# A residual of two adapted layers on Trainium2: adapter stack of 128 rows, first token sums and halves earlier, late adapter terms in other banks

## The chip, the cores and the metric

The kernel is written by hand, with a queue of instructions for each engine, and runs on one core of a Trainium2 chip. A core has TensorE (PE, with its weight loads shown as PEld), VectorE (DVE), ScalarE (ACT), GpSimd (POOL) and SyncE (SP), which here only issues DMAs. They meet at semaphores. The metric is the device time of one execution in microseconds (us), lower is better.

## The reference

Two layers, each added to its input. The first is a linear layer whose weight is quantised in groups of 128 against a codebook of 8 levels, with a low-rank term on both sides of the quantisation; the second is a gated MLP with an adapter chosen for each sequence.

```python
def layer0(x, weight, scale_log, codebook, lora_A, lora_B):       # weight 1024 x 1024, rank 64
    lora_delta = lora_B @ lora_A * (32.0 / 64.0)
    cb = codebook / clip(max(abs(codebook)), 1e-08)
    scale = exp(scale_log)
    normalized = (weight + lora_delta).reshape(O, I // 128, 128) / scale
    thresholds = (cb[:-1] + cb[1:]) * 0.5
    quantized = cb[searchsorted(thresholds, normalized, side='left')]
    w_eff = (quantized * scale).reshape(O, I) + lora_delta
    return x @ w_eff.T

def layer1(x, W_gate, W_up, W_down, A_*, B_*, lora_indices):      # H 1024, F 2752, rank 16, 16 adapters
    def lora_add(base, inp, A, B):
        Ab, Bb = A[0][lora_indices], B[0][lora_indices]           # one adapter for each of 8 sequences
        t = einsum('bri,bni->bnr', Ab, inp)
        return base + einsum('bor,bnr->bno', Bb, t) * 0.5
    gate = lora_add(x @ W_gate.T, x, A_gate, B_gate)
    up = lora_add(x @ W_up.T, x, A_up, B_up)
    act = silu(gate) * up
    return lora_add(act @ W_down.T, act, A_down, B_down)

x = x + layer0(x, ...)          # x is 8 x 256 x 1024, float32
x = x + layer1(x, ...)
```

## The kernel before

**The three stages.** Operands are split in two parts, high and low (names ending in h and l, as `xh`, `xl`), and each product is three matmuls: high by high, low by high, high by low. The token axis of 2048 is cut in NC = 4 pieces of 512, the feature axis of 1024 in KD = 8 tiles of 128. The first stage, up to about 239 us of the profiled span, quantises the eight row blocks of the first weight on VectorE (`quantise(o)`), transposes them on PE and makes 32 main products (`main(i)`, L1876), one for each block o and token piece c, in the order of the list ORDER. ScalarE copies each out of PSUM (`out_x1(i)`), and SyncE stores it to XR_d in DRAM (`store_x1(i)`). Product 26, for (7, 0), is LAST0, and 27, for (7, 1), is LAST1: their results go straight into the token tile `xr` too (L1095). The main products end at 239 us.

The second stage, 239 to 1190 us, makes gate and up by a scheme of seven products of half size in place of eight. A step u is one of them: mm = u // 7 counts the blocks of 128 output features (44 of them, gate and up in turn: m = mm % 2), p = u % 7 is the product. Each product is 12 matmuls of 512 columns (L1744). The scheme needs sums of token halves (`x_sum(n)`, L1323, four of them, from raw loads of XR_d into seven slots of `xr`) and sums of weight pieces (on GpSimd). `OUT` gives the PSUM bank of each product: bank1, bankA's second and first half, bank7, bank5, bankC's second and first half. `take(mm, p)` on VectorE reads them after products 2, 3, 4 and 6 of a block (L1269 to L1285), four reads in all, into `ev`. The stage runs twice, for tokens of halves h = 0 (u = 0 to 153) and h = 1 (u = 154 to 307). The third stage, 1190 us to the end, multiplies with W_down by the same scheme (L1967), reading its operands back from DRAM.

**The adapters.** The adapter projections of the tokens, `ts`, and the adapters' other factors, `bs`, are stacked in three groups of CR = 32 rows: one matmul with 96 rows adds the term to a product's bank (`lora`, L1760; 160 of them). In the first block pair of each half `ts` is not ready in time, as it comes from the first reads of PSUM themselves (`ts_mask`, L1341, L1348). There the terms are made later in banks of their own and added on VectorE (`late_lora`, L1768; `late_add`, L1355; 16 in all): before products 6, 7, 8, 9 and 13 to 16 of the half, in bank7, bank5 and the two halves of bankC. `td` (L1785) makes the down-projection's adapter term from `ah` and `al`, the high and low part of the activations, and `ad`.

**What sets the order.** Each engine's program is written out by hand. What stands behind a waiting instruction on an engine waits too; this holds for SyncE's and ScalarE's DMA issues. Between the first two stages the order matters most. BdT_d in DRAM holds an adapter matrix transposed in eight blocks; ScalarE copies a block from PSUM into the one buffer `bd_st` (`bd_copy(o)`, L1102) and may do so only when SyncE's store of the block before (`store_bd(o)`, L676) has landed. `load_raw` (L508) loads tokens from XR_d into slots of `xr`; `load_wn` and `load_wa` bring the rows of W_gate and W_up and their adapter rows; `w_tr(mm, n)` transposes them on VectorE, `hi(v)` and `lo(v)` split the weights of product v on ScalarE and VectorE (L951, L1245), `x_hi` and `x_lo` those of the tokens (L964, L1254), and `b_hi`, `b_lo` those of `bs`.

**The head.** `lb` holds a block of lora_B. SyncE loads lb(0) as its second load; PE transposes it (`lb_group(0)`, L1799), VectorE makes `lbT` of it and only then computes the thresholds from the codebook (from L1480). PE multiplies `la` by `lbT` (`lora_delta`, L1809), adds, transposes the quantised weights (`w_groups`, L1845) and the tokens (`nat_group`, L1828), and ScalarE and VectorE split both (`lxh`, `lxl`; `lwh`, `lwl`).

## Time and profile before

| | |
|---|---|
| Time, median of 3 runs | 1616.69 us (1616.1 to 1617.36) |
| The profiled execution's own time | 1616.32 us |
| Span of the profiled execution | 1614.7 us |
| PE busy | 1576.9 us, 98% of the span |
| DVE, ACT, POOL busy | 1275.1, 564.9 and 529.0 us |
| DMA | 257.13 MB, 159 GB/s in the mean |

The span goes from the first to the last instruction in the trace of one execution. All times within the profile are us from the span's start. The other times are of executions without a profile. Busy shares are means over three stages; what bounds a stage is read from the stage. A row of the page or the trace names the engine, the line in the kernel, the operation, the tile written, `<-`, and the tiles read. A wait in brackets is the engine's idle time just before the row, with what ended it.

### The profile page before, as it was taken

The page shows a single profiled execution, that of the slowest core. Times are in us where ns is not written, and L with a number is a line of the kernel's source. Part 1 is how long each engine was busy: PE and PEld are TensorE (multiplying, and loading weights), DVE is VectorE, ACT ScalarE, POOL GpSimd, SP SyncE. Part 2 cuts the span into 40 slices and gives each one's busy share as a digit, 9 for nine tenths or more (in the row PEclk, how much of TensorE's full clock was granted, in tenths as well). Part 3 has the DMA queues.
Part 4 walks back from the last instruction along what each step waited for, and adds up shares of the span by engine and source line. Part 5 has one row for each costly group of instructions (what it writes and reads, how often), then busy time and mean ns, then how long its engine had stood idle before and what let it go on. Part 6 is the DMA issues. An engine that isn't in the chain of part 4 may idle for free.

```text
span 1614.7 us, 21155 instructions
## 1 busy us (share of the span) xinstructions
PE 1576.9 (98%) x6968; PEld 1293.7 (80%) x6968; DVE 1275.1 (79%) x1674; ACT 564.9 (35%) x990; POOL 529.0 (33%) x399
## 2 busy tenths in 40 slices
PE   6999998999999999997999999999999999999999
PEld 4888886788888888876788888888888888888887
DVE  7998959988878988889887889989775576785443
ACT  6411134433333333354333333333343333233231
POOL 4410013455555555543444555555410000000000
PEclk9999999999999999999999999999999999999999
DMA  9552162565667777682446777776367777686563
GB/s 296 121 112 77 52 200 44 137 168 154 163 149 170 180 178 173 164 289 69 108 103 139 181 178 179 180 180 156 82 205 205 163 182 191 147 227 205 155 189 119
DMA packets 362444, 257.13 MB, mean 159 GB/s; under 512 B 219616, under 2 KB 283360, under 8 KB 362208
## 3 DMA queue, kind: packets, MB, share of 16 engines
q1 hardware_dynamic: 278784, 220.99, 52.2%
q10 hardware_dynamic: 81472, 28.99, 7.4%
q0 software_dynamic: 2080, 5.80, 1.7%
q8 instruction: 57, 0.93, 0.2%
q14 instruction: 51, 0.42, 0.1%
HBM read 165.74 MB, written 87.26 MB: 157 GB/s over the span
## 4 chain that ended last, share of the span: by engine, by line
PE 50%; DVE 1%; issue 0%; DVEq 0%
PE bank L1744 10%; PE bank L1967 9%; PE bankC L1967 6%; PE bankA L1744 6%; PE bankC L1744 6%; PE bankA L1967 6%; PE bankT L1967 3%; PE bankT L1785 1%; PE bankT L1786 1%; PE bankC L1760 1%; DVE ql L1417 0%; PE bank L1760 0%; PE bankA L1760 0%; DVE ev L1365 0%; DVE ll L1423 0%; DVE rl L1245 0%
## 5 line engine op out<-in xcount | busy, mean ns | idle before, releaser
L951 ACT CAST rh<-wt 128x512 fp32r<-128x512 f32 x308 | 190.7, 621 | 435.2 <-PE bankC L1760 127.7
L1245 DVE TENSOR_TENSOR rl<-wt,rh 128x512 fp32r<-128x512 f32 x308 | 274.0, 894 | 9.5 <-ACT rh L951 9.1
L1423 DVE TENSOR_TENSOR ll<-ll,lh 128x512 fp32r<-128x512 f32 (+1 forms) x154 | 107.8, 701 | 155.3 <-ACT lh L1060 155.0
L1744 PE MATMUL bank<-xh,rh 128*128 128x512 f32 x528 | 206.2, 391 | 1.1 <-issue 1.1
L1744 PE MATMUL bank<-xl,rh 128*128 128x512 f32 x528 | 205.8, 390 | 0.0
L1744 PE MATMUL bank<-xh,rl 128*128 128x512 f32 x528 | 205.7, 390 | 0.0
L1060 ACT CAST lh<-ll 128x512 fp32r<-128x512 f32 (+1 forms) x154 | 95.6, 621 | 268.6 <-DMA ll<-LT_d 263.5
L817 POOL TENSOR_TENSOR wt<-wt 128x512 f32<-128x512 f32 x44 | 60.1, 1365 | 321.6 <-DVE wt L1239 321.6
L1744 PE MATMUL bankC<-xh,rh 128*128 128x512 f32 x352 | 140.0, 398 | 3.1 <-DVE xl L1254 1.8
L1239 DVE STREAM_TRANSPOSE wt<-wn 128x512 f32<-128x512 f32 x176 | 124.1, 706 | 20.9 <-DMA wn<-Ag_d 9.0
L1744 PE MATMUL bankC<-xl,rh 128*128 128x512 f32 x352 | 139.5, 396 | 0.0
L1744 PE MATMUL bankC<-xh,rl 128*128 128x512 f32 x352 | 139.3, 396 | 0.0
L1744 PE MATMUL bankA<-xl,rh 128*128 128x512 f32 x352 | 137.0, 389 | 0.0
L1744 PE MATMUL bankA<-xh,rl 128*128 128x512 f32 x352 | 137.0, 389 | 0.0
L1744 PE MATMUL bankA<-xh,rh 128*128 128x512 f32 x352 | 137.0, 389 | 0.0
L1744 PEld LDWEIGHTS bank<-xh,rh 128*128 128x128 f32 x528 | 99.2, 188 | 23.1 <-issue 1.9
L1744 PEld LDWEIGHTS bank<-xl,rh 128*128 128x128 f32 x528 | 99.3, 188 | 21.2
L1744 PEld LDWEIGHTS bank<-xh,rl 128*128 128x128 f32 x528 | 99.1, 188 | 21.2
L830 POOL TENSOR_TENSOR wt<-wt 128x512 f32<-128x512 f32 x44 | 64.1, 1456 | 151.7 <-issue 91.2
L1269 DVE TENSOR_TENSOR ev<-bankA,tm 128x1024 f32<-128x1024 f32 x44 | 53.3, 1211 | 47.3 <-PE bankA L1760 45.7
L1967 PE MATMUL bank<-ql,lh 128*128 128x512 f32 (+1 forms) x231 | 90.0, 389 | 0.0
L1967 PE MATMUL bank<-qh,lh 128*128 128x512 f32 (+1 forms) x231 | 89.9, 389 | 0.0
(205 smaller groups left out, 3570.3 us busy)
## 6 DMA issues: line engine op xcount, KB each, us to landing
ll<-LT_d SPq DMA_DIRECT2D x148, 256.0 KB, 2.9
wn<-in_L_cond_W_gate_dram SPq DMA_DIRECT2D x80, 256.0 KB, 5.2
wn<-in_L_cond_W_up_dram SPq DMA_DIRECT2D x80, 256.0 KB, 5.1
RT_d<-dt SPq DMA_DIRECT2D x70, 256.0 KB, 3.2
ql<-RT_d SPq DMA_DIRECT2D x70, 256.0 KB, 3.8
LT_d<-ev ACTq DMA_DIRECT2D x60, 256.0 KB, 2.5
dn<-in_L_cond_W_down_dram SPq DMA_DIRECT2D x86, 128.0 KB, 3.8
LT_d<-s2a SPq DMA_DIRECT2D x40, 256.0 KB, 4.3
```

What stands on the lines that cost most here:

```text
L817: tt(wsrc(S1, rows), wsrc(L21, rows), wsrc(L22, rows), ALU.add).then_inc(s_sum, 1)
L830: tt(wsrc(L12, rows), wsrc(L12, rows), wsrc(S2, rows), ALU.subtract).then_inc(s_sum, 1)
L951: nc.scalar.copy(rh[:, v % RING, 0:KH * rows], wsrc(RSRC[p], rows)).then_inc(s_hi, 1)
L1060: nc.scalar.copy(lh[0:rows, n % NL, :], ll[0:rows, n % NL, :].bitcast(f32)).then_inc(s_lh, 1)
L1239: dv.transpose(wsrc(n, rows), src).then_inc(s_tr, 1)
L1245: dv.tensor_tensor(rl[:, v % RING, 0:KH * rows], wsrc(RSRC[p], rows), rh[:, v % RING, 0:KH * rows].bitcast(f32), ALU.subtract).then_inc(s_ ...
L1269: dv.tensor_tensor(e[:, 0:2, :], bankA[r, :, :], tm[r, None, :].to_broadcast([r.stop, 2, CH]), ALU.add).then_inc(s_ev, 1)
L1423: dv.tensor_tensor(ll[0:rows, n % NL, :], ll[0:rows, n % NL, :].bitcast(f32), lh[0:rows, n % NL, :].bitcast(f32), ALU.subtract).then_inc(s ...
L1744: last = te.matmul(OUT[p], a[:, u % RING, cols], b[:, OPND[p], k, :], start=k == 0 and n == 0, stop=k == KH - 1 and n == 2 and (p in (0, 1 ...
L1760: te.matmul(OUT[p][0:rows, :], bs[0:3 * CR, m, t, half * rows:(half + 1) * rows], ts[0:3 * CR, t, m, :], start=False, stop=True).then_inc( ...
L1785: te.matmul(bankT[:, :], lhs, ah[0:rows, :], start=begin, stop=False)
L1967: last = te.matmul(out_, a[0:rows, n % NL, tok], b[0:rows, k, :], start=(k == 0 and i == 0), stop=(k == NJ - 1 and i == 2))
```

## The change

It has five parts.

1. **Stack of 128 rows.** `lora` and `late_lora` multiply all 128 rows of `ts` and `bs`. Rows 96 to 127 are set to zero once, by GpSimd, at step u = 1; the first late term waits for it (semaphore s_z).
2. **Head.** lb(0) is loaded on ScalarE's queue, ahead of all else on it, instead of SyncE's. VectorE computes the thresholds before it makes lbT. PE does `w_groups(0)` before `lora_delta(1)`, and VectorE splits the first block's weights at the beginning of the next `quantise` instead of after its scaling.
3. **Seam between stage one and two.** The numbering of the token sums changes so that the first sum needs LAST0 alone, not LAST1. SyncE issues three raw loads before the store of BdT block 6. ScalarE asks for the first adapter rows earlier, and splits products 3 and 4 earlier; VectorE likewise, ahead of the first token sum, and transposes two weight pieces of block 1 before the token splits.
4. **Late terms.** They come before products 8, 9, 11, 12 and 14 to 17 of the half, the first four in bankC and bankA. The first activations' silu is at product (1, 6) instead of (1, 4), and copies, splits and `td` of the first block pair come one product later.
5. **Stage three** keeps its operands in one pair of tiles, `oph` and `opl`, with tables L_AT and R_AT for the places; what is read and multiplied stays.

The core of the diff:

```diff
+        LATE_BANK = ((bankC[0:FH, 1, :], bankC[0:FH, 0, :], bankA[0:FH, 1, :], bankA[0:FH, 0, :]),
+                     (bank7[0:FH, :], bank5[0:FH, :], bankC[0:FH, 1, :], bankC[0:FH, 0, :]))
+        LATE_AT = {8: (0, 0), 9: (0, 1), 11: (0, 2), 12: (0, 3), 14: (1, 0), 15: (1, 1), 16: (1, 2), 17: (1, 3)}
...
-        XORD = R11, T2, R21, T3, T1, T4, R22 = range(7)
+        XORD = R11, T2, R21, T3, T1, T4, R22 = (0, 4, 2, 3, 1, 5, 6)
@@ SyncE @@
-                load_lb(0)
...
-                store_bd(KD - 2)
-                stored(sp, TURN[KD - 2, 1] + 1)
+                stored(sp, KH * NC)
                 load_raw(0, 0, KH, 0, s_x[0])
                 load_raw(1, 0, KH, 3, s_x[3])
+                stored(sp, TURN[KD - 2, 0] + 1)
+                load_raw(0, KH, KD - 1, 2, s_x[2])
+                store_bd(KD - 2)
                 store_x1(LAST1)
+                stored(sp, TURN[KD - 2, 1] + 1)
                 load_raw(1, KH, KD - 1, 6, s_x[6])
-                load_raw(0, KH, KD - 1, 2, s_x[2])
+                load_wn(1)
                 store_bd(KD - 1)
                 store_x1(TURN[KD - 2, 2])
-                load_wn(1)
@@ GpSimd @@
+                    if u == 1:
+                        stored(gp, NORD)
+                        gp.wait_ge(s_bdst, 16 * KD)
+                        gp.wait_ge(s_sum, 4)
+                        gp.memset(ts[3 * CR:P, :, :, :].bitcast(f32), 0.0).then_inc(s_z, 1)
+                        gp.wait_ge(s_z, 2)
+                        gp.memset(bs[3 * CR:P, :, :, :].bitcast(f32), 0.0).then_inc(s_z, 1)
@@ ScalarE @@
+                for i in range(NI):
+                    act.dma_start(lb[i * Q:(i + 1) * Q, :, :],
+                                  lora_B[i * DI:i * DI + Q, None, :].to_broadcast([Q, 2, RL])).then_inc(s_lb0, 16)
...
                                 w_hi(o)
+                                if o == KD - 1:
+                                    load_wa(0)
...
                 bd_copy(KD - 2)
-                load_wa(0)
                 hi(0)
                 out_x1(LAST0)
                 hi(1)
                 out_x1(LAST1)
+                x_hi(0, 0)
                 bd_copy(KD - 1)
                 b_hi(0)
                 hi(2)
+                hi(3)
+                hi(4)
                 load_wa(1)
                 out_x1(TURN[KD - 2, 2])
-                x_hi(0, 0)
-                hi(3)
@@ VectorE @@
-                        dve.wait_ge(s_main, LAST1 + 1)
+                        dve.wait_ge(s_main, LAST0 + 1)
...
                 lo(2)
+                lo(3)
+                lo(4)
                 x_sum(0)
                 x_lo(0, 0)
                 for n in range(1, 4):
                     x_sum(n)
+                w_tr(1, 0)
+                w_tr(1, 1)
@@ PE @@
-                te.matmul(OUT[p][0:rows, :], bs[0:3 * CR, m, t, half * rows:(half + 1) * rows], ts[0:3 * CR, t, m, :],
+                te.matmul(OUT[p][0:rows, :], bs[:, m, t, half * rows:(half + 1) * rows], ts[:, t, m, :],
...
+                    if h == 0 and m == 0:
+                        pe.wait_ge(s_z, 3)
-                    pe.wait_ge(s_ev, 4 * 2 * NJ * h + 4 * m + (2, 3, 4, 4)[i])
+                    pe.wait_ge(s_ev, 4 * 2 * NJ * h + ((4, 4, 5, 5), (6, 7, 8, 8))[m][i])
...
-                lora_delta(1)
                 w_groups(0)
+                lora_delta(1)
...
-                    if first(it) and 7 * m + p in (6, 7, 8, 9, 13):
-                        late_lora(h, (7 * m + p - 6) // 7, (7 * m + p - 6) % 7)
-                    if it % NJ == 1 and m == 0 and p < 3:
-                        late_lora(h, 1, p + 1)
+                    if u % (14 * NJ) in LATE_AT:
+                        late_lora(h, *LATE_AT[u % (14 * NJ)])
```

**SyncE's DMA issues at the first seam.** XR_d<-x1t_st stores a main product, BdT_d<-bd_st a block of BdT, and xr<-XR_d is a raw load. Before:

```order
L681 DMA XR_d<-x1t_st 128x512 [waits s_x1t]
L676 DMA BdT_d<-bd_st 128x128 [waits s_bd]
L508 DMA xr_93<-XR_d 128x4x512 [waits s_x1tst1,s_x1tst0]
L508 DMA xr_93<-XR_d 128x4x512
L681 DMA XR_d<-x1t_st 128x512 [waits s_x1t]
L508 DMA xr_93<-XR_d 128x3x512 x2
L676 DMA BdT_d<-bd_st 128x128 [waits s_bd]
L681 DMA XR_d<-x1t_st 128x512 [waits s_x1t]
```

Now:

```order
L683 DMA XR_d<-x1t_st 128x512 [waits s_x1t]
L511 DMA xr_93<-XR_d 128x4x512 [waits s_x1tst1,s_x1tst0]
L511 DMA xr_93<-XR_d 128x4x512
L511 DMA xr_93<-XR_d 128x3x512 [waits s_x1tst1,s_x1tst0]
L678 DMA BdT_d<-bd_st 128x128 [waits s_bd]
L683 DMA XR_d<-x1t_st 128x512 [waits s_x1t]
L511 DMA xr_93<-XR_d 128x3x512 [waits s_x1tst1,s_x1tst0]
L468 DMA wn_97<-in_L_cond_W_up_dram 32x3x256 [waits p1_tr]
```

The store of BdT block 6 has moved from before the first raw load to behind the third, and the four loads now stand in the order of slots 0, 3, 2, 6.

**ScalarE at the same seam.** bd_st<-bankC is the copy of a block of BdT, rh<-wt a weight split, x1t_st<-bank the copy of a main product, xh<-xr a token split, wn<-Au_d the request for adapter rows. Before, from the copy of product (7, 1) on:

```order
L1095 COPY xr_93<-bankT 128x512 [waits s_x1tst1,s_main]
L1096 COPY x1t_st<-bankT 128x512
L1102 ACTIVATE bd_st<-bankC 128x128 [waits s_bdst,s_trM]
L983 ACTIVATE bh<-bt 128x192 [waits p1_bt]
L951 CAST rh<-wt 128x512 [waits p1_tr]
L974 DMA wn_97<-Au_d 32x2x256 [waits p1_tr]
L974 DMA wn_97<-Au_d 32x2x256 x3
L1096 COPY x1t_st<-bank 128x512 [waits s_x1tst0,s_main]
```

Now:

```order
L1110 COPY xr_93<-bankT 128x512 [waits s_x1tst1,s_main]
L1111 COPY x1t_st<-bankT 128x512
L976 CAST xh_91<-xr_93 128x1024 [waits p1_x0]
L976 CAST xh_91<-xr_93 128x1024
L1117 ACTIVATE bd_st<-bankC 128x128 [waits s_bdst,s_trM]
L995 ACTIVATE bh<-bt 128x192 [waits p1_bt]
L963 CAST rh<-wt 128x512 [waits p1_tr]
L963 CAST rh<-wt 128x512 [waits p1_sum] x2
L986 DMA wn_97<-Au_d 32x2x256 [waits p1_tr]
L986 DMA wn_97<-Au_d 32x2x256 x3
L1111 COPY x1t_st<-bank 128x512 [waits s_x1tst0,s_main]
```

The first token split stands ahead of the last copy into bd_st, and two more weight splits (x2) ahead of the adapter rows and the main product's copy.

**PE around the first late term**, from the last three matmuls of product 5 of the half. Before:

```order
L1744 MATMUL bankC<-xh_91,rh 128x512
L1744 MATMUL bankC<-xl_92,rh 128x512
L1744 MATMUL bankC<-xh_91,rl 128x512
L1768 MATMUL bank<-ts,bs 96x512 [waits p1_bs0,p1_ev,p1_tlo,p1_ts]
L1744 MATMUL bankC<-xh_91,rh 128x512 [waits p1_xlo,p1_lo]
L1744 MATMUL bankC<-xl_92,rh 128x512
L1744 MATMUL bankC<-xh_91,rl 128x512
```

Now, that place and the first late term, which comes behind product 7 (bank<-xh,rh and so on):

```order
L1764 MATMUL bankC<-xh_91,rh 128x512
L1764 MATMUL bankC<-xl_92,rh 128x512
L1764 MATMUL bankC<-xh_91,rl 128x512
L1764 MATMUL bankC<-xh_91,rh 128x512 [waits p1_xlo,p1_lo]
L1764 MATMUL bankC<-xl_92,rh 128x512
L1764 MATMUL bankC<-xh_91,rl 128x512
L1764 MATMUL bankC<-xh_91,rh 128x512
```

```order
L1764 MATMUL bank<-xh_91,rh 128x512
L1764 MATMUL bank<-xl_92,rh 128x512
L1764 MATMUL bank<-xh_91,rl 128x512
L1790 MATMUL bankC<-ts,bs 96x512 [waits p1_bs0,p1_tlo,p1_ev,p1_ts,p1_z]
L1764 MATMUL bankA<-xh_91,rh 128x512 [waits p1_ev,p1_lo]
L1764 MATMUL bankA<-xl_92,rh 128x512
L1764 MATMUL bankA<-xh_91,rl 128x512
```

The matmul of ts and bs has gone from before product 6 to before product 8, writes bankC instead of bank (bank7), and has one wait more (p1_z).

## Rows read from the trace of the kernel before

**Rows 1.** The page, part 1: busy us of each engine, share of the span, instructions.

```profile
PE 1576.9 (98%) x6968; PEld 1293.7 (80%) x6968; DVE 1275.1 (79%) x1674; ACT 564.9 (35%) x990; POOL 529.0 (33%) x399
```

**Rows 2.** Waits, whole span: engine, line, waited for: us, times, longest us.

```profile
ACT bd_st L1102 <- DMA BdT_d<-bd_st: 9.4, 2, 7.5
...
PE bank L1768 <- DVE ts L1348: 9.2, 2, 5.9
...
PE bankC L1799 <- DMA lb<-in_L_cond_lora_B_dram: 9.1, 1, 9.1
...
PE bankT L1785 <- DVE al L1329: 3.8, 4, 1.6
...
PE bank L1768 <- ACT ts L1000: 0.6, 1, 0.6
```

**Rows 3.** Windows: length, busy us (instructions) of five engines, granted clock, DMA share, GB/s.

```profile
34.00:36.00 2.00, 1.41 (x3) 1.16 (x4) 0.50 (x2) 0.00 (x0) 0.00 (x0) 0.54 1.05 379
262.90:266.20 3.30, 3.29 (x8) 2.62 (x9) 3.24 (x5) 1.35 (x3) 0.00 (x0) 0.50 0.26 43
```

**Rows 4.** Windows, two stretches of steady matmuls, same columns.

```profile
820.00:1020.00 200.00, 200.00 (x879) 165.01 (x878) 170.46 (x223) 70.43 (x125) 101.41 (x70) 1.00 0.69 157
1300.00:1500.00 200.00, 200.00 (x882) 165.41 (x882) 139.88 (x223) 66.99 (x115) 0.00 (x0) 1.00 0.70 188
```

**Rows 5.** Timeline of PE around a 96-row matmul: start us, us.

```profile
848.23 0.40 PE L1760 MATMUL bank<-ts,bs 96*128 96x512 f32 x1
...
849.16 0.39 PE L1744 MATMUL bankC<-xh,rh 128*128 128x512 f32 x1
```

**Rows 6.** Timeline of the head, ScalarE and PE: waits stand in brackets.

```profile
33.27 0.59 ACT L1081 CAST lxl<-bankC 128x512 fp32r<-128x512 f32 x1
...
34.59 2.08 PE L1809 MATMUL bank<-la,lbT 128*128 128x512 f32 x4 [1.36 <-DVE lbT L1457]
...
40.07 0.47 PE L1876 MATMUL bank<-lxh,lwh 128*128 128x512 f32 x1 [1.15 <-DVE lwl L1575]
```

**Rows 7.** Timeline of SyncE's queue, its DMA issues at the seam.

```profile
216.74 0.97 SPq L508 DMA_DIRECT2D xr<-XR_d  x2
...
220.45 0.99 SPq L508 DMA_DIRECT2D xr<-XR_d  x2
...
221.49 0.51 SPq L676 DMA_DIRECT2D BdT_d<-bd_st  x1
```

**Rows 8.** Tile BdT_d, 190 to 240 us: time from issue to landing.

```profile
DMA to landing us min/median/max: 2.1/2.1/10.7
```

**Rows 9.** Tile xr, 210 to 240 us: time from issue to landing.

```profile
DMA to landing us min/median/max: 5.9/9.6/11.1
```

**Rows 10.** Timeline of the first seam, by time, several engines.

```profile
211.66 0.39 PE L1876 MATMUL bankT<-lxh,lwh 128*128 128x512 f32 x1
...
214.71 0.58 ACT L1095 COPY xr<-bank 128x512 f32<-128x512 f32 x1
...
219.60 0.53 POOL L912 MEMSET ad<- 128x512 f32 x1
...
219.93 0.29 ACT L1102 ACTIVATE bd_st<-bankC 128x128 f32<-128x128 f32 x1
...
227.11 2.29 DVE L1323 TENSOR_TENSOR xr<-xr 128x2048 f32<-128x2048 f32 x1 [5.40 <-DMA xr<-XR_d]
...
268.51 1.23 DVE L1285 TENSOR_TENSOR ev<-bankC,ev 128x1024 f32<-128x1024 f32 x1
...
270.75 0.40 PE L1744 MATMUL bankA<-xh,rh 128*128 128x512 f32 x1
```

**Rows 11.** Timeline of the second half's seam, VectorE and PE.

```profile
734.88 3.67 DVE L1254 TENSOR_TENSOR xl<-xr,xh 128x1024 fp32r<-128x1024 f32 x2
...
748.43 1.23 DVE L1285 TENSOR_TENSOR ev<-bankC,ev 128x1024 f32<-128x1024 f32 x1
...
750.99 0.40 PE L1744 MATMUL bankA<-xh,rh 128*128 128x512 f32 x1
```

More of the change, by code:

```diff
@@ L735, in _ @@
                     late_b = it % NJ in (0, 1)
-                    if m == 0 and 0 < it < NIT and p == (3 if it % NJ == 1 else 0):
+                    if m == 0 and 0 < it < NIT and p == (4 if it % NJ == 1 else 0):
                         store_bs(it, 1)
@@ L1167, in _ @@
                         a_hi(4 * it)
-                    if 0 <= it - 1 < NIT and first(it - 1) and (m, p) == (0, 1):
+                    if 0 <= it - 1 < NIT and first(it - 1) and (m, p) == (0, 2):
                         a_hi(4 * (it - 1))
@@ L1965, in _ @@
                         out_ = BANK2[r % 2][t]
-                        for i, (a, b) in enumerate(((lh, qh), (lh, ql), (ll, qh))):
-                            last = te.matmul(out_, a[0:rows, n % NL, tok], b[0:rows, k, :],
+                        for i, (a, b) in enumerate(((oph, oph), (oph, opl), (opl, oph))):
+                            last = te.matmul(out_, a[0:rows, L_AT[n % NL], tok], b[0:rows, R_AT[k], :],
                                              start=(k == 0 and i == 0), stop=(k == NJ - 1 and i == 2))
```

107 lines of the change are left out of this document (55 added, 52 removed).

## The prediction

> **What bounds the kernel now.** I read the page's busy shares first: TensorE (PE) is busy for 98% of the span [rows 1], so a gain is a gap of PE closed, a clock kept up, or a cheaper matmul. The list of waits says where PE stands still: 9.1 us until lora_B lands at the start, and 9.2 us in two pieces (the longer 5.9) for the small adapter operand ts at the first late term of each half; further down 3.8 us for al; and ScalarE waits 9.4 us in two pieces for a store of BdT [rows 2]. The windows show that gaps of PE cost twice: after them the granted clock was 0.54 of full in 34 to 36 us and 0.50 for 3.3 us from 262.9, the lower level, 1.2 instead of 2.4 GHz [rows 3]. Last I compared PE's rate in two stretches without a wait: 882 matmuls in 200 us of the last matrix product, 879 in 200 us of the first, where the adapter products are [rows 4].
>
> **Change 1: the adapter product on 128 rows instead of 96.** After the 96-row matmul at 848.23 four starts take 0.93 us, to 849.16 [rows 5]; at the plain rate of 200/882 = 0.2268 us they would take 0.907: 0.023 us lost. The two rates agree with that: 3 matmuls x 0.2268 = 0.68 us in 200 us, over some 38 adapter products, is 0.018 each, and the last product has 96-row steps of its own that lose some as well; I take 0.025. There are 160 regular and 16 late adapter products: 176 x 0.025 = 4.4 us (bounds 0, if the loss hangs on something else in these matmuls, and 5). The Trainium skill ("TensorE: Matmul & The Clock Gate", LDWEIGHTS) says that a 32x128 weight load takes as long as a 128x128 one, only columns count. By that rule this part is worth nothing; the trace doesn't decide on the load, but shows starts that slip behind the matmul.
>
> **Change 2: the head.** lora_B now leads ScalarE's queue, and VectorE makes its constants while it travels, instead of after it. Four issues fewer stand ahead of the codebook on SyncE, and the first quantisation should end some 2.5 us earlier. But PE's next work also needs ScalarE's splits of the tokens, which end at 33.27 + 0.59 = 33.86 [rows 6]: these, not VectorE, will be last. The tokens come four issues (some 0.5 us each, as on SyncE [rows 7]) later on ScalarE's queue, and today PE waits for them a little; so 33.86 slips by up to 1 us. Today four delta matmuls and 16 transposes run from 34.59 to about 39, at half clock, and the first main matmul comes at 40.07, after a wait of 1.15 for VectorE's last split of the weights [rows 6]. With the quantised weights there earlier, their transposes and that split go ahead of the delta. I take 40.07 - 1.15 for the wait that goes, less 0.7 of today's 1.36 ahead of 34.59: 38.2, a gain of 1.8 us (bounds -0.5, the tokens' delay, and 2.9, both waits and 0.4). PE is busy without a gap worth naming from there to 239 us, so the shift is kept.
>
> **Change 3: the seam between the two layers (200 to 313 us).** Here VectorE decides. The first token sum starts at 227.11, when its two loads land, and VectorE is never idle from there to the end of the fourth PSUM read at 268.51 + 1.23 = 269.74: 42.6 us [rows 10]. The change takes two weight splits out of this stretch (1.2 us), leaving 41.4, and starts the loads when main product (7,0) is done, at 211.66 [rows 10]. Today ScalarE copies it at 214.71, behind a cast that waits for weight transposes, and these for the adapter rows, whose request now goes out earlier. From that copy to the load's issue at 216.74 [rows 7] are 2.03 us, 0.5 of it the BdT store between: 211.7 + 0.3 + 1.5 gives 213.6, 3.1 us earlier.
> What SyncE's order shows speaks against the gain: the store of BdT (o = 6), which stood ahead of the loads, now stands behind three of them. A BdT store with little ahead landed in 2.1 us, the one issued at 221.49 behind the loads in 10.7 [rows 7, 8]. ScalarE's next copy into bd_st waits for that store, and ScalarE works in order. The last load, issued at about 220.97, took 11.1 [rows 7, 9], so 3.5 MB went from 216.74 to about 232.1, 4.4 us per MB; the three ahead of the store are 2.75 MB: 213.6 + 12.1 = 225.7, the store at 226.3. Today that copy ran at 219.93 [rows 10]. Queued behind it on ScalarE are b_hi(0), hi(2), hi(3), hi(4), the next adapter rows and out_x1. Who waits: VectorE's b_lo(0), lo(2), lo(3), lo(4), all ahead of the first sum, and through out_x1(28) PE's main product 30. After the copy (0.3) come a cast of 0.4 and three of 0.5, and one split (0.7): the first sum starts at 229.0, 1.9 us later than today. If ScalarE weren't held it would start with its loads at 213.6 + (227.11 - 216.74) = 224.0.
> From 229.0, 41.4 us of VectorE's work: 270.4. The new zeroing of ts and bs on GpSimd (512 elements took 0.53 us [rows 10]; 3072 make some 3.2) runs beside it and may slow VectorE by 0 to 1.6; I take 0.5: 270.9. PE now needs exactly this read before the late term ahead of product 8, so that product starts at 271.2 where today it is 270.75 [rows 10]: 0.45 lost. The wait ahead of product 6 is gone, but PE stands about as long ahead of 8, and the half clock then falls on work that nothing hides: a spell of 3.3 us [rows 3] loses up to half its length, I take 1.2 us. Behind product 8 there are gains: the silu no longer stands ahead of the adapter copies on ScalarE (0.6, the third wait for ts [rows 2]), and the down-projection terms come one product later, which covers 1.6 of the 3.8 us for al [rows 2]. Sum: -0.45 - 1.2 + 0.6 + 1.6 = 0.6 gained (bounds -3 and 6.5).
>
> **Change 4: the same seam in the second half (712 to 790 us).** No load moves. Today PE waits 5.9 us for ts [rows 2]; now product 6 starts when its token split ends, 734.88 + 3.67 = 738.6 [rows 11]. But VectorE's chain to the read at 748.43 + 1.23 = 749.66 stays, and the late term now waits for it: product 8 starts at 749.9 instead of 750.99 [rows 11], 1.1 gained. The gap of 5.9 becomes one of 3.5 and one near 5, after which I expect the half clock once where nothing hides it (1.4, a little more, the gap being longer). Behind it one wait for al of the four (0.9) and some slack at the late terms (0.4): 1.1 + 1.3 - 1.4 = 1.0 us (bounds -1.5 and 3).
> The tiles of the last product only change places; nothing of their order moves: 0.
>
> **Sum**, against the profiled execution's own 1616.32 us (span 1614.7 and 1.6 around it): -4.4 - 1.8 - 0.6 - 1.0 = -7.8, so 1608.5. It lies 0.4 under the median of the timed runs (1616.69), so **1608.9**.
>
> **Rivals.**
> - A, the forecast: ScalarE is held by the BdT store. For it: 10.7 against 2.1 us [rows 8]. Chance 0.45.
> - B: the store lands in time, or little waits for it. The first sum starts at 224.0, 5.0 us earlier: 1603.9. Against it: the two landings. Chance 0.25.
> - C: the 96 rows are not what makes the starts slip; the 4.4 are missing: 1613.3. Against it: the slip sits right behind the 96-row matmul [rows 5]. This is also what the skill's rule, quoted above, would give. Chance 0.13.
> - D: the head gives nothing or loses 0.5, since the tokens land late behind lora_B, with the hold of A: 1610.7 to 1611.2. Chance 0.12.
> - E, slower: the hold of ScalarE grows. Place: the copy of BdT (o = 7) into bd_st. Price: one us of the whole for each us of landing past 226, for main product 30, all sums and the splits stand behind it. To eat 7.8 and 3.2 more the store must land after 237, which 2.75 MB do only at half of today's rate: 1620. Chance 0.05.
>
> The range 1602.5 to 1613.5 leaves out E, half of C and the best of B. This kernel's measurement tells about 0.2% (3.2 us) from no change, so faster means under 1613.5. A (0.44 of 0.45), B (0.25), half of C (0.06) and most of D (0.10) are faster: 0.85; the rest of C and D and an edge of A 0.10; slower 0.05.
>
> **What would show it.** In the profile after: starts behind adapter matmuls at 0.227 us, and as many matmuls per 200 us as in the last product (else C). First main matmul at 37.5 to 39, no wait of 9 us. ScalarE's copy into bd_st waiting for a BdT store until about 224.5, the first sum near 227 (B: near 222), both 1.8 under the clock of before by the head, then a wait of PE for the PSUM read ahead of the first late term. In the second half a wait of PE that ends near 749.9 less the total shift. I would be wrong if main matmuls wait earlier than 200 us, or if the waits for al and ad grow.

## The result, and the profile after

The changed kernel takes 1629.98 us (median of 4 runs, 1629.51 to 1631.03); the kernel before, run beside it, 1617.03. The ratio is 1.0081 (95% interval 1.0066 to 1.0096): 13 us slower, where I had forecast 8 us faster. In the profiled executions it is 1630.23 against 1616.32 us, 13.9 more, and their spans differ by as much:

```profile
span 1628.6 us, 21162 instructions
...
PE 1577.9 (97%) x6968; PEld 1295.6 (80%) x6968; DVE 1273.3 (78%) x1674; ACT 565.1 (35%) x990; POOL 526.8 (32%) x401
```

PE is busy 1.0 us more than before [rows 1] and stands still 12.9 us more; stretches at half clock count as busy. The starts of the products of stage two, read from PE's timelines, say where (a stretch ends with the start of the product named last, the rest with the span):

| stretch, by products u of stage two | its end before, us | its end after, us | lost (+) or gained (-) |
|---|---|---|---|
| to product 0: head and main products | 239.02 | 243.43 | +4.4 |
| 0 to 8 | 270.75 | 274.77 | -0.4 |
| 8 to 21 | 312.66 | 321.68 | +5.0 |
| 21 to 154, no seam | 714.40 | 721.67 | -1.7 |
| 154 to 162, start of the second half | 750.99 | 757.57 | -0.7 |
| 162 to 182 | 812.95 | 828.62 | +9.1 |
| 182 to 307, no seam | 1186.80 | 1200.62 | -1.9 |
| rest, stage three | 1614.7 | 1628.6 | +0.1 |

So there are three losses: one in the head, and one behind product 8 of either half. In the two stretches without a seam the change gains. PE's waits in the profile after name the same places (us in total, times, longest; "issue" is a wait for nothing that the profile shows):

```profile
PE bankT L1807 <- DVE al L1346: 9.9, 6, 3.4
...
PE bankA L1853 <- DMA nat<-in_x_dram: 6.8, 2, 5.5
...
PE bankC L1824 <- DMA lb<-in_L_cond_lora_B_dram: 6.5, 1, 6.5
...
PE bankC L1790 <- DVE ev L1302: 6.4, 2, 3.9
...
PE bankC L1764 <- issue: 4.5, 2, 3.2
```

The wait for lora_B fell from 9.1 [rows 2] to 6.5, but 6.8 us for `nat`, the tokens, are new. The waits for ts are gone and 6.4 us for `ev`, the read of PSUM, stand in their place. Those for `al` grew from 3.8 [rows 2] to 9.9.

**The head.** The queues of ScalarE and SyncE, and PE's first token transposes (start, duration, and in brackets the idle time and what ended it):

```profile
0.94 1.81 ACTq L1075 DMA_DIRECT2D lb<-in_L_cond_lora_B_dram  x4
...
4.68 1.01 ACTq L1080 DMA_DIRECT2D nat<-in_x_dram  x2
...
4.06 0.98 SPq L649 DMA_DIRECT2D nat<-in_x_dram  x2
...
16.48 1.08 PE L1853 MATMUL bankA<-ident,nat 128*128 128x128 f32 x4 [5.52 <-DMA nat<-in_x_dram]
...
40.03 1.88 PE L1870 MATMUL bankA<-ident,eff 128*128 128x128 f32 x8 [0.77 <-ACT lxl L1096]
...
44.26 0.47 PE L1901 MATMUL bank<-lxh,lwh 128*128 128x512 f32 x1
```

ScalarE's two loads of the first token piece went out at 4.68, behind eight other issues (2.77 in the kernel before), and SyncE's loads of the second piece already at 4.06 (6.00 before). These are the times from issue to landing of ScalarE's two loads after:

```profile
DMA to landing us min/median/max: 11.7/14.1/16.5
```

The first of them took 7.9 us before; it landed at 10.7 then and lands at 16.4 now, and PE stood 5.5 us for it. SyncE's first load landed at about 13.8, ahead of it. ScalarE's splits end at 39.9 instead of 33.9 us, and the first main product starts at 44.26 instead of 40.07 [rows 6].

**Behind product 8.** SyncE's queue, VectorE and PE in the first half:

```profile
262.19 1.80 SPq L472 DMA_DIRECT2D wn<-in_L_cond_W_gate_dram  x4
...
291.01 1.15 SPq L507 DMA_DIRECT2D bs<-bh  x2
...
294.73 2.07 SPq L472 DMA_DIRECT2D wn<-in_L_cond_W_up_dram  x4
...
295.71 0.68 DVE L1365 TENSOR_TENSOR ts<-tx,ts 32x512 fp32r<-32x512 f32 x1 [3.35 <-ACT ts L1011]
...
302.33 0.71 DVE L1256 STREAM_TRANSPOSE wt<-wn 128x512 f32<-128x512 f32 x1 [3.82 <-DMA wn<-in_L_cond_W_up_dram]
...
313.00 0.61 PE L1807 MATMUL bankT<-ah,ad 96*128 96x512 f32 x1 [3.36 <-DVE al L1346]
```

The stores into bs (L507, six DMAs that refill bs) wait for the late terms' additions of the first block, as those terms still read bs. It is by far SyncE's longest wait from 262 to 303 us (the kernel before has two there, the longer of 19.1 us):

```profile
SPq L502 <- DVE ev L1372: 26.9, 1, 26.9
```

The last of these additions now comes with product 12 instead of 9, and the stores go out at 291.01 where they went at 278.57 before. Behind them on SyncE stands the load of the next block of W_up: 294.73 where it was 282.29. VectorE's transposes wait 3.8 us for it, until 302.33, and all that VectorE has behind them is late: PE then waits 3.4 us for `al`. In the second half it is the same, and more: VectorE waits 5.9 us.

```profile
DVE wt L1256 <- DMA wn<-in_L_cond_W_up_dram: 9.7, 2, 5.9
...
DVE ts L1365 <- ACT ts L1011: 4.1, 2, 3.3
```

The same list of the kernel before has no wait for W_up. Its queue of SyncE at this place:

```profile
278.57 1.15 SPq L504 DMA_DIRECT2D bs<-bh  x2
...
282.29 2.06 SPq L469 DMA_DIRECT2D wn<-in_L_cond_W_up_dram  x4
```

**What came as forecast.** ScalarE's copy into bd_st waited for the store of BdT, which took 9.5 us from its issue at 219.38 to its landing, and the first token sum came behind it:

```profile
228.93 0.28 ACT L1117 ACTIVATE bd_st<-bankC 128x128 f32<-128x128 f32 x1 [3.65 <-DMA BdT_d<-bd_st]
...
233.06 2.28 DVE L1340 TENSOR_TENSOR xr<-xr 128x2048 f32<-128x2048 f32 x1
```

The starts behind an adapter matmul do not slip any more, and both stretches without waits now hold 883 matmuls in 200 us, where they held 879 and 882 [rows 4]:

```profile
820.00:1020.00 200.00, 200.00 (x883) 165.29 (x882) 169.30 (x223) 70.64 (x127) 100.75 (x70) 1.00 0.69 160
...
1300.00:1500.00 200.00, 200.00 (x883) 165.45 (x882) 142.25 (x228) 66.31 (x113) 0.00 (x0) 1.00 0.71 190
```

And PE's timeline around one of them, four starts in 0.91 us where it was 0.93 [rows 5]:

```profile
849.29 0.39 PE L1780 MATMUL bankC<-ts,bs 128*128 128x512 f32 x1
...
850.20 0.39 PE L1764 MATMUL bank<-xh,rh 128*128 128x512 f32 x1
```

The weight load of these matmuls (PEld; busy us, then mean ns of one) takes the same time with 96 rows, in the kernel before, as with 128 rows now:

```profile
L1760 PEld LDWEIGHTS bankC<-ts,bs 96*128 96x128 f32 x80 | 15.0, 188 | 3.1
...
L1780 PEld LDWEIGHTS bankC<-ts,bs 128*128 128x128 f32 x80 | 15.0, 188 | 3.1
```

### The profile page after: what moved, and what is told of

It reads as the page before. It is cut to its first block, busy times and chain, and to the rows that moved or that the text cites. A ratio compares the mean times of both kernels' runs of the same rounds, so it can differ in the third digit from the quotient of the medians.

```text
span 1628.6 us, 21162 instructions
## 1 busy us (share of the span) xinstructions
PE 1577.9 (97%) x6968; PEld 1295.6 (80%) x6968; DVE 1273.3 (78%) x1674; ACT 565.1 (35%) x990; POOL 526.8 (32%) x401
## 4 chain that ended last, share of the span: by engine, by line
PE 49%; DVE 1%; SPq 0%; DMA 0%; issue 0%; DVEq 0%
PE bank L1991 9%; PE bank L1764 9%; PE bankC L1991 6%; PE bankA L1991 6%; PE bankA L1764 6%; PE bankC L1764 6%; PE bankT L1991 3%; PE bankT L1807 1%; PE bankT L1808 1%; PE bankC L1780 1%; DVE opl L1433 0%; DMA bs<-bt 0%; PE bank L1780 0%; PE bankA L1780 0%; DVE opl L1439 0%; DVE ev L1381 0%
## 5 line engine op out<-in xcount | busy, mean ns | idle before, releaser
L1439 DVE TENSOR_TENSOR opl<-opl,oph 128x512 fp32r<-128x512 f32 (+1 forms) x154 | 107.4, 698 | 155.5 <-ACT oph L1072 155.2
L1072 ACT CAST oph<-opl 128x512 fp32r<-128x512 f32 (+1 forms) x154 | 95.5, 621 | 268.5 <-DMA opl<-LT_d 263.5
L1991 PE MATMUL bank<-opl,oph 128*128 128x512 f32 (+1 forms) x231 | 90.0, 390 | 0.0
L1991 PE MATMUL bank<-oph 128*128 128x512 f32 (+1 forms) x231 | 89.9, 389 | 0.0
```

The lines of the kernel that those rows point to most:

```text
L1072: nc.scalar.copy(oph[0:rows, L_AT[n % NL], :], opl[0:rows, L_AT[n % NL], :].bitcast(f32)).then_inc(s_lh, 1)
L1439: dv.tensor_tensor(opl[0:rows, L_AT[n % NL], :], opl[0:rows, L_AT[n % NL], :].bitcast(f32), oph[0:rows, L_AT[n % NL], :].bitcast(f32), ALU ...
L1991: last = te.matmul(out_, a[0:rows, L_AT[n % NL], tok], b[0:rows, R_AT[k], :], start=(k == 0 and i == 0), stop=(k == NJ - 1 and i == 2))
```

## The experiments

All ratios are against runs of the kernel before on the same chip, with 95% intervals. The kernel before took 1616.1 us in the median beside experiments 1 to 4, 1616.8 beside 5 to 8 and 1616.0 beside 9 to 11, so across these groups the ratios compare better than the times.

| | time, us | ratio |
|---|---|---|
| changed kernel | 1629.98 | 1.0081 (1.0066 to 1.0096) |
| 1, weight load ahead of the stores of bs | 1620.94 | 1.0024 (1.0015 to 1.0033) |
| 2, lora_B on SyncE | 1625.52 | 1.0056 (1.0042 to 1.0070) |
| 3, late terms at their old places | 1617.47 | 1.0008 (0.9999 to 1.0017) |
| 4, kernel before with 128 rows alone | 1613.27 | 0.9981 (0.9972 to 0.9990) |
| 5, 2 and 3 together | 1614.64 | 0.9987 (0.9978 to 0.9996) |
| 6, 5 and the store of BdT ahead | 1609.30 | 0.9958 (0.9945 to 0.9972) |
| 7, 1 and the silu behind ts | 1618.72 | 1.0010 (1.0001 to 1.0019) |
| 8, four mends, late terms at new places | 1611.50 | 0.9964 (0.9950 to 0.9978) |
| 9, 6 with the old order in the head | 1610.06 | 0.9959 (0.9945 to 0.9972) |
| 10, 6 with lora_B on ScalarE, tokens in order | 1608.48 | 0.9953 (0.9939 to 0.9966) |
| 11, kernel before with the zeroing alone | 1616.91 | 1.0005 (0.9996 to 1.0014) |

**1. The weight load ahead of the stores of bs**, on SyncE alone:

```diff
-                    if m == 1 and it + 1 < NIT and p == (3 if late_b else 0):
-                        store_bs(it + 1, 0)
                     if p == 3 and 0 <= mm + 2 < NM:
                         load_wn(mm + 2)
+                    if m == 1 and it + 1 < NIT and p == (3 if late_b else 0):
+                        store_bs(it + 1, 0)
```

> The changed kernel, with one swap on SyncE: where both fall at the same step, the load of the block after next of W_gate or W_up is issued before the six stores of the adapter operand bs, not behind them. Theory (the stores wait for late terms that now come up to three products later, and the weight load behind them comes 12 us late, so VectorE stands 3.8 and 5.9 us for it): both of these waits go, the products behind number 8 of each half come 4 to 5 us and 7 to 8 us earlier, and the time falls by 9 to 12 us, from 1630 to 1618 to 1621. Rival 1 (the silu and the down-projection's operands, one to two products later in the order, are what is late): the waits of VectorE for weights go, but PE's waits for al stay at about 3 us each, and the time falls by less than 3 us. Rival 2 (the new banks of the late terms, reads of PSUM in the way): no change.

9.0 us came back by one swap of two steps. The load of W_up goes out at 284.64 and VectorE does not wait for it any more; PE waits for `al` 6.4 us in eight pieces:

```profile
284.64 2.01 SPq L472 DMA_DIRECT2D wn<-in_L_cond_W_up_dram  x4
...
290.67 1.15 SPq L507 DMA_DIRECT2D bs<-bh  x2
```

```profile
PE bankT L1807 <- DVE al L1346: 6.4, 8, 1.8
```

The wait in the queue is the cause of the greater part. In the profile 3.8 us come back from product 8 to 21 and 4.4 from 162 to 182, where I expected 4 to 5 and 7 to 8: the second half is still 4.7 us behind the kernel before in that stretch. So Rival 1 has a share; the 3.8 us for `al` of the kernel before are not reached either.

**2. lora_B back on SyncE**, first in its queue behind lora_A:

```diff
-                for i in range(NI):
-                    act.dma_start(lb[i * Q:(i + 1) * Q, :, :],
-                                  lora_B[i * DI:i * DI + Q, None, :].to_broadcast([Q, 2, RL])).then_inc(s_lb0, 16)
...
                 sp.dma_start(qsum[0:RL, :], lora_A).then_inc(s_la, 16)
+                for i in range(NI):
+                    sp.dma_start(lb[i * Q:(i + 1) * Q, :, :],
+                                 lora_B[i * DI:i * DI + Q, None, :].to_broadcast([Q, 2, RL])).then_inc(s_lb0, 16)
```

> The changed kernel, with the first block of lora_B loaded as second load on SyncE's queue again, as in the kernel before; the order on VectorE and PE stays the changed one. Theory (the four issues ahead of ScalarE's tokens and the earlier token loads of SyncE's queue hand the DMA engines to the wrong tokens first, so the first ones land at 16.3 instead of 10.7 us): the first tokens land at 10.5 to 12 us, the first main product starts at 39 to 40.5 instead of 44.3 us, and the time falls by 4 to 5.5 us, to 1624.5 to 1626. Rival (PE's and VectorE's new order in the head costs it: transposes of weights ahead of the low-rank product): the first main product stays later than 43 us and the time within 1.5 us of 1630.

1625.5, the theory's time, in the median of six executions. One of them, which is the profiled one, took 4094 us; without it the median is 1624.9. Its profile, with 0.83 us for a matmul throughout, is not used, and the head is read from experiments 5, 6 and 10. They show that this edit does more than its theory says: it also puts lora_B ahead of the codebook again (experiment 5).

**3. Late terms at their old places**: part 4 of the change undone, its core being

```diff
-        LATE_AT = {8: (0, 0), 9: (0, 1), 11: (0, 2), 12: (0, 3), 14: (1, 0), 15: (1, 1), 16: (1, 2), 17: (1, 3)}
+        LATE_AT = {6: (0, 0), 7: (0, 1), 8: (0, 2), 9: (0, 3), 13: (1, 0), 14: (1, 1), 15: (1, 2), 16: (1, 3)}
```

> The changed kernel with part 4 undone in full: late terms before products 6, 7, 8, 9, 13 to 16 in bank7, bank5 and bankC, the silu at (1, 4), everything of the first block pair at its old place; stack of 128 rows, head and seam stay. Theory: product 8 of the first half a little later (the wait ahead of product 6 returns), but no wait of VectorE for weights at 298 and 780 us, and the whole at 1616 to 1619 (1630 less 4.6 and 8.5 us, less the gain of 128 rows that was counted in them, plus nothing). Rival (the swap alone gives it all back and the late terms' new places are worth something for themselves): this run is 1 to 3 us slower than the one with the swap.

12.5 us came back, 3.5 more than by the swap: beside the queue, something else in part 4 costs. Experiment 7 finds 2.2 of it in the silu. And with the wait ahead of product 6 back, the first half shows no gain of the seam's new order against the kernel before: product 0 starts 4.4 us later than there, product 8 4.5 and product 21 4.4. (Experiment 4, which has 128 rows and the old seam, needs 1.1 us more from product 0 to 21 than this one, but that loss is not explained, so it shows no gain either.) PE's gap ahead of product 6 is 5.0 us:

```profile
267.46 0.71 PE L1791 MATMUL bank<-ts,bs 128*96 128x512 f32 x1 [4.96 <-ACT ts L1012]
```

**4. 128 rows alone** in the kernel before: the matmuls of `lora` and `late_lora` on 128 rows, the zeroing and the wait for it.

```diff
-                    te.matmul(OUT[p][0:rows, :], bs[0:3 * CR, m, t, half * rows:(half + 1) * rows], ts[0:3 * CR, t, m, :],
+                    te.matmul(OUT[p][0:rows, :], bs[:, m, t, half * rows:(half + 1) * rows], ts[:, t, m, :],
```

> The kernel before, with the stack of 128 rows alone (rows 96 to 127 zeroed on GpSimd at step 1, the first late term waits for it). Theory (each 96-row matmul makes the starts behind it slip by 0.025 us, 176 of them): 1617.0 - 4.4 = 1612.6. Rival (in the head and at the seams VectorE sets the pace and takes part of it back, or GpSimd's zeroing slows VectorE at the seam): 1613.5 to 1615.

Faster by 2.9 us; the time lies between the theory's 1612.6 and the rival's 1613.5, and the interval (1.6 to 4.5 us) holds both. The gain per matmul is as forecast: from product 28 to 150 the kernel makes up 1.85 us against the one before, over 70 adapter matmuls, 0.026 each. But over the first seam (products 5 to 21) it loses 1.1 us again, 0.7 of it from product 6 to 7, and over the second (158 to 182) 0.5. In experiment 11, with the zeroing alone, the profile does not show this loss.

**5. Experiments 2 and 3 together.**

> The changed kernel with part 4 (late terms) undone in full and the first block of lora_B back on SyncE's queue: what stays of the change is the stack of 128 rows, the new order of PE and VectorE in the head, and the seam between the first two stages. Theory (parts add up): 1617.5 - 4.5 = 1613.0, the first product of stage two at 238.7 to 239.5 us, and PE's gap ahead of product 6 as with part 4 undone alone, near 5 us: the seam's new order gives nothing, as ScalarE is held by the store of BdT. Rival (the head's new order gives 1 us or more once the tokens land as early as before): first product of stage two before 238 us, 1612 or less.

1614.6, between theory and kernel before. Product 0 starts at 240.7; in experiment 6, the same in the head, at 239.0; the kernel before had 239.0 too. So the head's new order of VectorE and PE shows no gain at product 0 in either. The tokens are not the reason: ScalarE's first load landed at 11.4 us (10.4 in experiment 6, 10.7 in the kernel before), and PE does not wait for it. The new order computes the constants from the codebook ahead of lbT, and with lora_B back on SyncE the codebook stands behind it in the queue. VectorE waits for the codebook, and PE for lbT (in the kernel before, 0.7 us, and the token transposes at 12.17):

```profile
10.58 0.17 DVE L1491 SCALAR_TENSOR_TENSOR cbt<-cb 128x8 f32<-128x8 f32 x1 [3.90 <-DMA cb<-in_condB_codebook_dram]
...
12.91 2.07 PE L1835 MATMUL bank<-la,lbT 128*128 128x512 f32 x4 [3.19 <-DVE lbT L1473]
...
14.78 1.05 PE L1854 MATMUL bankA<-ident,nat 128*128 128x128 f32 x4
```

Experiment 6 has the same two waits, 2.6 and 3.8 us. Its head is without the stretch at half clock that this one has: here the granted clock was 0.50 from 38.1 to 41.4 us, there 1.00 from 30 to 48. Behind the head, ScalarE is held as forecast, and the first sum late:

```profile
226.06 0.28 ACT L1117 ACTIVATE bd_st<-bankC 128x128 f32<-128x128 f32 x1 [3.63 <-DMA BdT_d<-bd_st]
...
230.05 2.28 DVE L1340 TENSOR_TENSOR xr<-xr 128x2048 f32<-128x2048 f32 x1
```

**6. The store of BdT ahead of the raw loads**, and the first token split behind the weight splits:

```diff
                 store_x1(LAST0)
+                store_bd(KD - 2)
                 stored(sp, KH * NC)
...
                 load_raw(0, KH, KD - 1, 2, s_x[2])
-                store_bd(KD - 2)
...
-                x_hi(0, 0)
                 bd_copy(KD - 1)
                 b_hi(0)
                 hi(2)
                 hi(3)
                 hi(4)
+                x_hi(0, 0)
```

> As the run with part 4 undone and lora_B on SyncE, with the store of BdT block 6 issued ahead of the three raw token loads instead of behind them, and on ScalarE the first token split behind the weight splits 2, 3 and 4 instead of ahead of the copy into bd_st. Theory (ScalarE's wait for that store holds the weight splits and so the first token sum): the copy into bd_st doesn't wait, the first sum starts at 223.5 to 225 instead of about 228.6 us, PE's gap ahead of product 6 shrinks from 5 to under 1.5 us, and the time is 1608 to 1610.5. Rival 1 (the token loads, not the hold, set the first sum): the sum starts no earlier than 227 us, 1612 to 1613.5. Rival 2 (the sum starts earlier, but the chain to ts and the reads of PSUM is paced by PE's products): the gap shrinks by less than half, 1611 to 1612.

1609.3: 5.3 us less, by the two edits together; what each gives is not separated. The copy into bd_st waits no more and stands at 218.26, the first sum starts at 222.48, 7.6 us earlier than in experiment 5 (1.7 of it the head), and product 8 at 267.36 instead of 273.46:

```profile
218.26 0.30 ACT L1117 ACTIVATE bd_st<-bankC 128x128 f32<-128x128 f32 x1
...
222.48 2.29 DVE L1340 TENSOR_TENSOR xr<-xr 128x2048 f32<-128x2048 f32 x1
...
229.55 2.29 DVE L1340 TENSOR_TENSOR xr<-xr 128x2048 f32<-128x2048 f32 x1 [2.39 <-DMA xr<-XR_d]
...
259.58 0.71 PE L1791 MATMUL bank<-ts,bs 128*96 128x512 f32 x1 [4.08 <-ACT ts L1015]
```

The gap ahead of product 6 is still 4.1 us, not under 1.5 as the theory had it (rival 2 had that right, though not the time): product 5 ends earlier too, as its waits for token splits (1.6 and 0.4 us in experiment 5) are gone. The second sum now waits 2.4 us for its load.

**7. The silu behind the casts of ts**, added to experiment 1:

```diff
-                        if (m, p) == (1, 6):
-                            for n in range(3):
-                                silu(it, n)
                         if p in (4, 6):
                             ts_hi(it // NJ, m, p // 6)
+                        if (m, p) == (1, 6):
+                            for n in range(3):
+                                silu(it, n)
```

> The changed kernel with the weight load ahead of the stores of bs on SyncE, as in the first experiment (1620.9), and on ScalarE the three silu of the first block pair behind the two casts of ts at the same step, not ahead of them. Theory (the table load and three silu hold the cast that VectorE waits 3.3 us for, and that delay comes out at PE's waits for al): VectorE's wait for ts of 3.3 us at 292 to 296 goes, PE's waits for al shrink from 6.4 us in sum to under 4, time 1618 to 1619.5. Rival (the waits for al come from the order, gating and split one product later on a VectorE that is full): no change, 1620 to 1621.5.

1618.7, 2.2 less than experiment 1, with a wide scatter (1614.8 to 1620.0, and 1618.1 to 1623.5 there) and ratios whose intervals just overlap. The profiles agree on the direction: 1.6 us less from product 8 to 21 and 2.9 less from 162 to 182. VectorE's wait of 3.3 us for ts is gone and PE's waits for `al` are 3.9 us, as the theory had it. So the silu did hold the casts of ts at its new place. With the swap and this the ratio is 1.0010, where experiment 3, with the late terms at their old places, has 1.0008: a cost of the new places beyond the queue and the silu is not shown in these two.

**8. All mends, late terms at their new places**: experiments 7, 2, and the edit of 6.

> The changed kernel with its late terms at their new places and four mends: weight load ahead of the stores of bs, silu behind the casts of ts, lora_B on SyncE, store of BdT block 6 ahead of the raw loads. Theory (the late terms' new places cost by themselves, because PE's wait ahead of product 6 is split in two, ahead of 6 and of 8, and the half clock after the second falls on products that nothing hides): 2 to 4 us slower than the run with the same mends and the late terms at their old places, 1611 to 1614. Rival (with the weights in time and ts early, two products more of slack for ts are a gain): as fast as that run or faster, under 1609.

1611.5, 2.2 slower than experiment 6 in the medians, though the intervals of the ratios overlap; in the profiles 3.4, of which 1.6 are the head. At product 160 it is ahead of experiment 6 by 2.0 us, at 162 behind by 0.9, at 182 by 3.5:

```profile
734.24 0.47 PE L1764 MATMUL bankC<-xh,rh 128*128 128x512 f32 x1 [3.18 <-issue]
...
739.49 0.67 PE L1807 MATMUL bankT<-ah,ad 128*128 128x512 f32 x1 [2.26 <-DVE al L1346]
...
745.39 0.44 PE L1790 MATMUL bankC<-ts,bs 128*96 128x512 f32 x1 [0.87 <-DVE ev L1302]
...
793.32 0.47 PE L1807 MATMUL bankT<-ah,ad 96*128 96x512 f32 x1 [1.95 <-DVE al L1346]
```

The windows behind the second and the last of them, where the granted clock (third number from the end) is half:

```profile
739.60:743.00 3.40, 3.40 (x9) 2.66 (x10) 3.27 (x5) 1.67 (x3) 2.00 (x2) 0.50 0.21 80
...
794.30:797.60 3.30, 3.30 (x9) 2.53 (x9) 3.17 (x6) 0.43 (x1) 1.49 (x2) 0.50 0.20 60
```

The one wait of 5.9 us is now 3.2, 2.3 and 0.9, and at 791 there is another of 1.9 for `al`; after two of them the clock falls to half for 3.4 us. The time is the theory's, but its reason, the wait split ahead of 6 and 8, is not borne out: from product 158 to 162, over the three pieces, this version takes 21.8 us (two late matmuls come behind them now), where experiment 6 with its one wait and 6.8 us at half clock takes 22.2. It loses 2.6 us behind that, from product 162 to 182, where the wait of 1.9 us and the second window at half clock stand; experiment 6 has waits of 0.4 and 0.9 us there and its clock is full. In the first half, from product 0 to 154, this version is 0.3 us faster.

**9. The old order in the head**, added to experiment 6 (constants behind lbT, `lora_delta(1)` ahead of `w_groups(0)`, the weight split behind the scaling).

> The best run so far (128 rows, late terms at their old places, lora_B on SyncE, store of BdT ahead of the raw loads: 1609.3) with the head of the kernel before in full: constants of VectorE behind lbT, low-rank product of block 1 ahead of the transposes of block 0's quantised weights, weight split behind the scaling. Theory (the first main products hang on the tokens' landing and ScalarE's splits, and the new order adds nothing, or loses up to 1.5 us because the low-rank product that the second quantisation needs comes later): 1608 to 1609.5. Rival (the new order gives what I forecast once the tokens are early, 1 to 2 us): this run is slower, 1610.3 to 1611.3.

1610.1 against 1609.3: no difference that can be told. The time lies between the theory's range (to 1609.5) and the rival's (from 1610.3), and the ratios are 0.9959 and 0.9958. In the profile product 0 starts 0.7 us later than in experiment 6. Both have lora_B on SyncE, where the new order waits for the codebook; with lora_B on ScalarE the old order was not tried.

**10. lora_B on ScalarE as in the change, the second token piece behind the scales**, on the base of experiment 6:

```diff
-                load_nat(2)
-                load_nat(3)
                 for i in range(NI):
                     sp.dma_start(scale[i * Q:(i + 1) * Q, 1:KD, :],
                                  scale_log[i * DI + Q:(i + 1) * DI].rearrange("(o r) g u -> r o (g u)", r=Q)).then_inc(s_scr, 16)
+                load_nat(2)
+                load_nat(3)
```

> The best run so far, but with lora_B on ScalarE's queue ahead of everything, as the change has it, and on SyncE's queue the loads of the second token piece behind the four loads of the remaining scales instead of ahead of them. Theory (the first tokens landed late because SyncE's token loads, issued at 4.06 instead of 6.0 us, got ahead of ScalarE's, issued at 4.68 instead of 2.77; with those out of the way only the 1.9 us of the four issues stay): the first tokens land at 11.5 to 13.5 us instead of 16.3, stage two starts at 238.5 to 241, time 1609 to 1611.5. Rival (the four issues ahead of ScalarE's tokens cost it all): first tokens at 15.5 us or later, stage two at 243 us, 1613 to 1614.5.

1608.5, and the profiled execution 1606.6. ScalarE's token loads still go out at 4.68, behind eight issues; with SyncE's at 6.00 instead of 4.06, the first of them lands at 10.9 instead of 16.4 us, and PE starts on it without a wait at 10.97 instead of 16.48. The rival had 15.5 or later. ScalarE's two loads took, and around them stood:

```profile
DMA to landing us min/median/max: 6.2/7.8/9.5
...
4.68 1.02 ACTq L1080 DMA_DIRECT2D nat<-in_x_dram  x2
...
4.06 1.89 SPq L654 DMA_DIRECT2D scale<-in_L_cond_scale_log_dram  x4
...
6.00 1.32 SPq L649 DMA_DIRECT2D nat<-in_x_dram  x2
...
10.97 1.08 PE L1854 MATMUL bankA<-ident,nat 128*128 128x128 f32 x4
```

Product 0 starts at 235.75, 3.3 us earlier than in the kernel before and in experiment 6, and earlier than the theory's 238.5 to 241. Here the codebook is there before lora_B, and VectorE waits for neither. In the medians only 0.8 us of that show, with overlapping intervals: that this head is no worse than the old one is shown, that it is better rests on one profiled execution.

**11. The zeroing alone**, with 96 rows.

> The kernel before with 96 rows, and only GpSimd's zeroing of rows 96 to 127 of ts and bs at step 1 and the wait of the first late term for it. Theory (the zeroing runs beside VectorE and ScalarE at the seam and costs there what the stack of 128 rows alone missed, 1.0 of 4.4 us): PE's gap ahead of product 6 near 5 instead of 3.2 us, product 21 at 313.5 instead of 312.7, time 0.8 to 1.5 us above the kernel before. Rival (the loss comes from the 128 rows or from scatter): no difference, within 0.4 us.

The times cannot tell: the median is 0.9 us above the kernel before's, within the theory's range, but the interval reaches from 0.6 us faster to 2.3 slower. The profile speaks for the rival: the shift of 0.3 to 0.5 us is there from product 0 on and does not grow at the seam, and PE's gap ahead of product 6 is 3.3 us, not near 5. What experiment 4 loses at the seams is not settled; its wait ahead of product 6 is 4.9 instead of 3.2 us, and the half clock lasts 6.8 us in one piece that begins within this wait, instead of twice 3.4, one of them ahead of the wait.

## Why the prediction was wrong

- **Change 1, 4.4 us: right in mechanism.** -1.7 and -1.9 in the two stretches without a seam, at 0.026 a matmul (I took 0.025). Alone it measured 2.9, as 1.1 and 0.5 us are lost at the seams. The Trainium skill ("TensorE: Matmul & The Clock Gate", LDWEIGHTS) says that a weight load's time goes by its columns, not by its rows. The traces agree: 188 ns with 96 and with 128 rows. I wrote that the trace does not decide on the load; it did. And I was wrong that by this rule the part is worth nothing: the time is lost in the starts behind the matmul, not in the load, and there 883 matmuls fit in 200 us instead of 879. Why the starts slip stays open.
- **Change 2, -1.8 us: wrong, +4.4.** The step that failed is "33.86 slips by up to 1 us": it slipped by 6.0, to 39.9. I counted the issues on ScalarE's queue and took the landing to move with them. But I had noted myself that SyncE's queue gets shorter, and used it only for the codebook: its token loads, two of 1 MB (512 x 512 float32) that PE needs later, went ahead of ScalarE's by the same 1.9 us. The first tokens landed 5.7 us later. Rival D had the mechanism's place and a size of 0.5. Experiment 2 takes the loss away by putting lora_B back (4.5 to 5.1 us), experiment 10 by putting the other tokens back instead; in its profile the head then gains 3.3 us, more than the 1.8 that I forecast.
- **Change 3 up to product 8, 0.45 lost: right in mechanism.** The hold of ScalarE by the store of BdT was there (copy at 228.9 less 4.4 of the head is 224.5, where I had 226.3), the first sum at 233.06 less 4.4 is 228.7 (229.0 forecast, though the terms behind 226.3 add up to 229.2), product 8 at 270.4 (271.2 forecast, so 0.4 gained instead). Experiment 6 takes the hold away and gains 5.3 us, near the 5.0 of rival B, but its second edit has a share that is not known. The zeroing, for which I took 0.5 us, shows no cost at this seam in experiment 11's profile.
- **Change 3 behind product 8, 2.2 us gained: wrong, 5.0 lost. Change 4, 1.0 gained: wrong, 8.4 lost.** The step that failed is "Behind product 8 there are gains". I never followed the late terms to SyncE's queue, where `store_bs` waits for their additions, and the load of the weights stands behind it. SyncE's order has these stores and their wait for the additions at almost the same place as before; a wait whose row stays in place still gets longer when what it waits for moves. Experiment 1 shows 9.0 us for it. The silu was the smaller miss: that it "no longer stands ahead" was true of the first casts of ts alone (experiment 7, 2.2). The waits for `al` were to shrink by 1.6 and 0.9 us; they grew from 3.8 to 9.9, which the prediction itself names as a sign of being wrong.
- **Change 4 up to product 162: right in mechanism, sizes off.** Product 162 starts 0.7 us earlier against product 154, where I had 1.1. The two waits are 3.2 and 2.4 us, where I had 3.5 and near 5. Half clock follows each of them for 3.4 us, where I had it once.
- The rivals were all about the hold of ScalarE, the tokens and the 96 rows. None took a queue that stands behind a moved consumer; E, the slower side, had another place and 0.05.

The version with the lowest median is experiment 10, not to be told from 6 and 9 by the times: 1608.5 us, 0.9953 (0.9939 to 0.9966) of the kernel before, with 128 rows, lora_B on ScalarE, tokens in order, BdT's store ahead, late terms at their old places.

## What to carry to other kernels

When work that reads a buffer is moved later, list every instruction on every queue that waits for this reading, and what stands behind each: here two swapped steps on SyncE were worth 9 us. When a queue gets shorter, ask which of its later transfers now overtake another queue's urgent one. When a load is moved back, ask what now stands behind it: here the codebook. A gain read from PE's waits is worth only what VectorE's and the queues' chain to the same point leaves of it.

## What the runs showed of the hardware

- When 1 MB of tokens on ScalarE's queue landed hung by more than 5 us on when SyncE's queue issued its own: with SyncE's two loads of 1 MB issued 0.6 us before ScalarE's, the first of ScalarE's landed at 16.4 (15.8 to 16.8 in experiments 1, 3 and 7, which have the same head); issued 1.3 us after them, at 10.9 (one profile, experiment 10).
- After a matmul with 96 rows the starts slip by 0.026 us in sum (1.85 us over 70 of them, experiment 4); after one with 128 rows they do not (849.29 to 850.20 for four). The weight load takes 188 ns with either.
- A store of 64 KB (BdT) that was issued behind three token loads landed after 9.5 us, where stores with little ahead of them landed after 2.1 [rows 8].
- At a granted clock of 0.50 the matmuls start 0.427 us apart (experiment 8, six steps from 794.83 to 797.39); at 1.00 it is 0.2265 (883 in 200 us). A stretch of 3.4 us at half clock so costs PE about 1.6 us, an estimate from these two rates, unless PE stands still in it.
